# Last group of a four-sublayer kernel: value products made slot by slot, last feed-forward, bias and store in two halves

## What is computed

```python
# xn = layernorm(x); 16 heads of 64
q, k, v = xn @ wq * 64**-0.5, ctx @ wk, ctx @ wv
x = x + softmax(q @ k.T + mask) @ v @ wo
x = x + relu(layernorm(x) @ w1 + b1) @ w2 + b2        # w1 128x512, w2 512x128
```

## Time and profile before

| | before |
|---|---|
| median of three runs | 1377.8 us |
| the profiled execution | 1374.36 us, span 1372.4 us |
| TensorE matmul busy | 1290.7 us, 94% of the span |
| VectorE, ScalarE, GpSimd busy | 72%, 57%, 38% |
| mean granted TensorE clock | 0.976 |
| scores of tile 60 begin, last matmul ends | at 1306.2 us, at 1369.2 us |

### The profile page before, as it was taken

The page is one execution under the profiler, slowest core; times in us unless marked ns, Lnnn a source line. Parts: engine busy times, 40 slices in busy tenths (PEclk is TensorE's granted clock), DMA queues, the critical chain, the costliest instruction groups (busy, mean ns, idle before and its releaser), DMA issues.

```text
span 1372.4 us, 41789 instructions
## 1 busy us (share of the span) xinstructions
PE 1290.7 (94%) x16144; PEld 1136.1 (83%) x16145; DVE 986.1 (72%) x2428; ACT 780.1 (57%) x1482; POOL 517.5 (38%) x557
## 2 busy tenths in 40 slices
PE   4899999996999999988999999999999999999976
PEld 3788888875999999976788888888888888888866
DVE  3688888866655555537788788878877887788673
ACT  3455556642655555546656665666666666666632
POOL 2266666654122222247344324432443344332000
PEclk9899999998899999999999999999999999999988
DMA  3123242211422222221110111011101110110000
GB/s 104 45 74 128 76 137 78 76 68 64 137 76 77 76 77 77 65 77 39 29 33 13 31 35 33 14 31 35 33 14 29 37 31 15 29 37 14 8 4 16
DMA packets 86510, 71.06 MB, mean 52 GB/s; under 512 B 25072, under 2 KB 73200, under 8 KB 86352
## 3 DMA queue, kind: packets, MB, share of 16 engines
q1 hardware_dynamic: 74752, 42.71, 10.9%
q0 software_dynamic: 11600, 26.10, 6.0%
HBM read 40.73 MB, written 28.05 MB: 50 GB/s over the span
## 4 chain that ended last, share of the span: by engine, by line
PE 39%; DVE 10%; issue 3%; ACT 2%; POOL 1%; DMA 0%; DVEq 0%; POOLq 0%; ACTq 0%
PE c_ps_w L83 17%; PE c_ps_w L1566 7%; PE c_ps_w L1583 4%; PE c_ps_s L1532 4%; PE c_ps_w L1555 3%; PE c_ps_w L1541 3%; DVE c_r_max L1944 2%; DVE c_shifted L1942 2%; DVE c_shifted L1945 2%; PE c_ps_w L1463 1%; DVE c_probs L1957 1%; DVE c_xn_t_low L1867 1%; DVE k_ctx_t_low L898 1%; ACT c_o_t L1747 1%; ACT c_q_t L1719 1%
## 5 line engine op out<-in xcount | busy, mean ns | idle before, releaser
L1376 POOL TENSOR_TENSOR c_rstd<-c_var,c_minus_half 128x1 f32<-128x1 f32 x64 | 35.7, 558 | 353.7 <-DVE c_var L1925 353.6
L92 POOL DMA_INDIRECT sorted_x<-a_xn,f_slot_of x128 | 128.4, 1003 | 92.4 <-PE a_ps_w L767 36.0
L1566 PEld LDWEIGHTS c_ps_w<-c_wo,c_o_t 128*128 128x128 f32 x1024 | 125.1, 196 | 33.9 <-ACT c_o_t L1747 27.1
L1566 PE MATMUL c_ps_w<-c_wo,c_o_t 128*128 128x128 f32 x1024 | 130.9, 282 | 20.7 <-ACT c_o_t L1747 20.6
L1350 POOL DMA_INDIRECT c_back<-sorted_y,k_y_row_of x112 | 110.9, 991 | 102.2 <-PE c_ps_w L1555 52.9
L1109 PE MATMUL d_ps_y<-e_w_all,d_h_t 128*128 x1136 | 138.7, 276 | 0.0
L1109 PEld LDWEIGHTS d_ps_y<-e_w_all,d_h_t 128*128 128x128 f32 x1136 | 133.6, 193 | 0.0
L980 POOL DMA_DIRECT2D sorted_y<-d_y_rows x71 | 50.8, 716 | 208.6 <-DVE d_y_rows L1011 204.3
L1942 DVE TENSOR_TENSOR c_shifted<-c_ps_s,c_mask 128x1024 f32<-128x1024 f32 x64 | 78.3, 1224 | 57.8 <-PE c_ps_s L1532 57.7
L1719 ACT ACTIVATE c_q_t<-c_ps_w 128x512 f32<-128x512 f32 x120 | 70.2, 602 | 85.7 <-PE c_ps_w L83 84.7
L1058 ACT ACTIVATE d_h_t<-d_ps_h,d_biases 128x256 f32<-128x256 f32 x284 | 112.0, 476 | 2.5 <-PE d_ps_h L83 2.0
(11 more groups left out here) (250 smaller groups left out, 3554.7 us busy)
## 6 DMA issues: line engine op xcount, KB each, us to landing
d_x_rows<-sorted_x SPq DMA_DIRECT2D x71, 128.0 KB, 2.1
sorted_y<-d_y_rows POOLq DMA_DIRECT2D x71, 128.0 KB, 2.2
k_X<-in_x SPq DMA_DIRECT2D x16, 256.0 KB, 3.0
a_q_rows<-in_ctx SPq DMA_DIRECT2D x16, 256.0 KB, 3.3
ctx_cols<-a_q_t SPq DMA_DIRECT2D x16, 256.0 KB, 2.0
k_ctx_raw<-ctx_cols SPq DMA_DIRECT2D x16, 256.0 KB, 2.8
out<-k_X SPq DMA_DIRECT2D x16, 256.0 KB, 3.1
sorted_x<-a_xn,f_slot_of POOLq DMA_INDIRECT x128, 2.2
```

The source lines that it names most:

```text
L92: pool.indirect_dma_start(out=sorted_x, out_offset=bass.IndirectOffsetOnAxis(ap=slot_of[:, choice, t:t + 1], axis=0), in_=xn2[:, k, :], in ...
L1566: last = pe.matmul(w[:, 0:D], o_t[:, j, :], wo[:, j, :], start=(j == 0), stop=(j == J - 1))
```

## The change

Four edits to the end of `phase_c`.

1. `project_v` of tiles 60 to 63 moves from slots 56 to 59 into slots 60 to 63: the first half (`v, p, 0`) ahead of `transpose_probs(p - 1)`, the second behind it. ScalarE's `take_v` moves likewise. Slot p then makes the values that slot p + 1 uses.
2. The feed-forward of group 15 is made in halves of two tiles. The first half's transposes ("x4a") go into slot 63 between `values(62)` and `out_projection(62)`, its up products ("upa": two banks with two products of 256 columns each, three passes a product) behind `transpose_probs(63)`, its down products behind `values(63)`, ahead of `out_projection(63)`. The second half ("x4b", "upb", down 1) comes last.
3. POOL adds the bias of the last group in two halves of 128x256, the first ahead of `root4(63)`.
4. SP stores the last group in two halves of 128 KB, each when its `finish` is done.

At the end of slot 56 TensorE has the pair for tile 60 behind `out_projection(55)`; slot 57 has the pair for tile 61, slot 58 for tile 62 (each one ahead of the projection and one behind it), slot 59 for tile 63 (both ahead of it).

The diff, cut to its core (the changes of `filled` and of the slot conditions repeat those of TensorE's loop):

```diff
@@ tensor, loop over slots
-                coming = g + 1 < G
+                coming, early, last = g + 1 < G, g + 2 < G, g + 1 == G
...
+                if last:
+                    project_v(p, (0,))
                 transpose_probs(p - 1)
+                if last:
+                    project_v(p, (1,))
...
+                if k == 1 and early:
                     project_v(p + GT, (0,))
...
-                if k == 3 and coming:
+                if k == 3 and early:
                     project_v(p + GT, range(2))
+                if k == 3 and last:
+                    last_transposes("x4a", 0)
                 out_projection(p - 1)
...
             transpose_probs(NT - 1)
+            last_up("upa", 0)
             values(NT - 1)
+            last_down(0)
             out_projection(NT - 1)
-            x4_transposes(G - 1)
-            feed_up(G - 1, range(HC))
-            for half in range(2):
-                feed_down(G - 1, half)
+            last_transposes("x4b", 1)
+            last_up("upb", 1)
+            last_down(1)
@@ tensor, new functions
+            def last_up(name, half):
+                emptied(("x4a", "x4b")[half], G - 1)
+                HW = GW // 2
+                for n in range(HC // 2):
+                    w = begin(name, G - 1, n)
+                    for a in range(2):
+                        j = 2 * n + a
+                        last = split_matmul(pe, w[:, a * HW:(a + 1) * HW], f1, xn_t, ...)
+                    last.then_inc(full, 1)
+            def last_down(half):
+                for n in range(HC // 2):
+                    emptied(("upa", "upb")[half], G - 1, n)
+                w = begin("down", G - 1, half)
+                for n in range(GT // 2):
+                    k = half * GT // 2 + n
+                    for j in range(HC):
+                        last = pe.matmul(w[:, n * D:(n + 1) * D], h_t[:, j, k * P:(k + 1) * P], f2[:, j, :], ...)
+                last.then_inc(full, 1)
@@ scalar
             take_probs(NT - 1)
+            take_last_hidden("upa", 0)
             take_values(NT - 1)
-            high_x4(G - 1)
-            take_hidden(G - 1, range(HC))
+            high_last("x4b", 1)
+            take_last_hidden("upb", 1)
+            def take_last_hidden(name, half):
+                act.wait_ge(full, full_at("down", G - 2, 1))
+                for j in range(HC):
+                    act.wait_ge(full, full_at(name, G - 1, j // 2))
+                    ins = act.activation(h_t[:, j, half * HW:(half + 1) * HW], ..., ACT.Relu, bias=fb1[:, j:j + 1])
+                    if j % 2 == 1:
+                        ins.then_inc(free_of(name, G - 1, j // 2), 1)
@@ vector
+                if k == 3 and g + 1 == G:
+                    low_last("x4a", 0)
                 add_attention(p - 1)
             normalise_x4(NT - 2)
+            finish(G - 1, 0)
             add_attention(NT - 1)
             normalise_x4(NT - 1)
-            low_part("x4", G - 1)
-            for half in range(2):
-                finish(G - 1, half)
+            low_last("x4b", 1)
+            finish(G - 1, 1)
@@ gpsimd
+            add_last_bias(0)
             root4(NT - 1)
-            add_bias(G - 1)
+            add_last_bias(1)
@@ sync
+            for half in range(2):
+                sp.wait_ge(y_ready, 2 * (G - 1) + half + 1)
+                ks = ds(GT * (G - 1) + half * GT // 2, GT // 2)
+                sp.dma_start(x_out[:, ks, :], X[:, ks, :]).then_inc(stored[(G + 1) % 2], 16)
```

More of the change, by code:

```diff
@@ L1216, in filled @@
             yield from (("pt", NT - 1, half) for half in range(2))
+            yield from (("upa", G - 1, n) for n in range(HC // 2))
             yield from (("pv", NT - 1, b) for b in range(NB))
+            yield ("down", G - 1, 0)
             yield ("o", NT - 1)
-            yield ("x4", G - 1)
-            yield from (("up", G - 1, j) for j in range(HC))
-            yield from (("down", G - 1, half) for half in range(2))
+            yield ("x4b", G - 1)
+            yield from (("upb", G - 1, n) for n in range(HC // 2))
+            yield ("down", G - 1, 1)
         def filled_in_slot(p):
             g, k = divmod(p, GT)
-            coming = g + 1 < G
+            coming, early, last = g + 1 < G, g + 2 < G, g + 1 == G
             if k == 0 and coming:
@@ L1255, in filled_in_slot @@
                 yield ("k", g + 1, 7)
+            if k == 2 and early:
                 yield ("v", p + GT, 0)
@@ L1263, in filled_in_slot @@
                 yield ("q", g + 1, 6)
+            if k == 0 and early:
                 yield from (("v", p + GT, h) for h in range(2))
-            if k in (1, 2) and coming:
+            if k in (1, 2) and early:
                 yield ("v", p + GT, 1)
@@ L1280, in free_at @@
             return NUMBER[name] // BANKS + 1
-        HIGHS = {name: n for n, name in enumerate(n for n in NUMBER if n[0] in ("xna", "xnb", "xn", "x4"))}
+        HIGHS = {name: n for n, name in enumerate(n for n in NUMBER if n[0] in ("xna", "xnb", "xn", "x4", "x4a", "x4b"))}
         block = ctx.enter_context(nc.Block())
@@ L1809, in _ @@
                     take_k(g + 1, (5, 6))
+                if last:
+                    take_v(p, (0,))
                 take_probs(p - 1)
+                if last:
+                    take_v(p, (1,))
                 if k == 0 and coming:
@@ L1842, in _ @@
                     high_ctx(g + 2)
+                if k == 3 and last:
+                    high_last("x4a", 0)
                 if k == 0 and coming:
                     take_q(g + 1, (6,))
+                if k == 0 and early:
                     take_v(p + GT, range(2))
-                if k in (1, 2) and coming:
+                if k in (1, 2) and early:
                     take_v(p + GT, (1,))
             take_probs(NT - 1)
+            take_last_hidden("upa", 0)
             take_values(NT - 1)
-            high_x4(G - 1)
-            take_hidden(G - 1, range(HC))
+            high_last("x4b", 1)
+            take_last_hidden("upb", 1)
         @block.vector
@@ L1915, in normalise_x, with low_last @@
                 normalise_rows(range(GT), GT * g)
+            def low_last(name, half):
+                dve.wait_ge(high_ready, HIGHS[name, G - 1] + 1)
+                cols = slice(half * GW // 2, (half + 1) * GW // 2)
+                dve.tensor_tensor(xn_t.low[:, cols], bank(name, G - 1)[:, 0:GW // 2], xn_t.high[:, cols],
+                                  ALU.subtract).then_inc(free_of(name, G - 1), 1)
             def add_attention(p):
```

40 lines of the change are left out of this document (33 added, 7 removed).

## The result

The changed kernel has a median of 1369.49 us over six runs (1367.7 to 1374.0), against 1378.11 for the kernel before (1377.33 to 1380.77, six runs): ratio 0.9936, interval 0.9917 to 0.9954. A second comparison gave 0.9943 (0.9930 to 0.9956). The forecast was 1368.9, with 1365.6 to 1372.9 around it.

The account below looks back on a forecast made before the run. TensorE bounds slots 56 to 59; later the softmax chain and half clock after holes do, then a serial tail. Terms -4.3 -1.0 -0.5 -0.8 +0.5 -0.35 -2.2 -0.2 = -8.9 us, median 1377.8 to 1368.9, range 1365.6 to 1372.9.

Parts of the forecast that it names:

- slots 56 to 59: Value products leave busy TensorE: saves 1.40, 1.40, 1.35 and 0.15 us, sum 4.3; slot 59 gets a 1.3 us hole.
- slot 60: Added products cost nothing, half the clock's gain returns: -1.0 us; sign: slots 60 and 61 are 9.1 to 9.9 long.
- slot 61: Added products cost nothing; half the gain from losing its cold scores is taken: -0.5 us.
- slot 62: Added products cost nothing; its partly cold projection becomes warm, whole gain taken: -0.8 us, bounds 0 and -0.8.
- slot 63: TensorE sets the time: pays 1.40, regains 0.85 by warm scores; +0.5 us, bounds +0.5 and +1.4.
- mid: End of tile 62's projection to end of tile 63's: TensorE without holes, warm, 7.4 us; -0.35, bounds -0.5 and +1.5.
- last: Last projection to the end, before the store: 10.4 us against 12.57 before; -2.2, bounds -1.8 and -4.8.
- store: Last add's end to span's end, store halved to 128 KB: -0.2 us, bounds 0 and -0.9.
- that rival: Slots 56 to 58 give little back: VectorE sets the pace, each saves 0.2, sum -5.4 us, 1372.4; chance 0.06.
- the softmax chain: Scores, VectorE passes, exponential, o_t copies, projection: no slot shorter than 9.07 us; added products lie beside it in slots 60 to 62.
- The two near rivals: All warm before the tail, warm down half: -11.6 us, 1366.2, chance 0.15; clock stays as it is: -5.05, 1372.7, 0.15.
- The slower one: Moved products lie in the late slots' path: +3.9 us, 1381.7; decides where the hole ahead of projection is below 1.4; chance 0.02.

Follow-up runs that it names:

- the variant with real products: Changed kernel with the last group's value products one tile ahead, in the holes: 98.4 us from tile 56's scores, ratio 0.9890 to the kernel before.
- the halves alone: Changed kernel without the value products' move, group 15's feed-forward, bias and store in halves: 109.0 us from tile 56's scores, ratio 0.9978 to the kernel before.
- the two variants with the products one ahead: Changed kernel, last group's value products one tile ahead, without and with down halves waiting later: 98.4 and 97.9 us from tile 56's scores, ratios 0.9890 and 0.9896.
- The late wait variant: Changed kernel, last group's down halves waiting for the second bank's relu only at the third hidden chunk: 101.8 us from tile 56's scores, ratio 0.9923.

## Why the prediction was right

The mechanism came out as forecast: what leaves TensorE where it never idles is given back, what is added where it idles costs nothing, slot 63 pays, and the clock decides the rest. The closeness of the medians, -8.6 measured for -8.9 forecast, is in part luck: the trace has -7.6, and the steps below miss it in both directions.

Step by step, forecast against the profile (difference to before):

| step | forecast | profile |
|---|---|---|
| slots 56 to 59 | -4.3 | -4.1 |
| slot 60 | -1.0 | -0.3 |
| slot 61 | -0.5 | -0.8 |
| slot 62 | -0.8 | -0.7 |
| slot 63 | +0.5 | +0.6 |
| mid | -0.35 | -0.5 |
| last | -2.2 | -1.4 |
| store | -0.2 | -0.4 |
| sum | -8.9 | -7.6 |

- **Slots 56 to 58.** TensorE was the bound, and what left it left the slot: 1.39, 1.36, 1.29. Slot 59 gave 0.09, the o_t copies being next, with a new hole of 1.26 against the 1.3 forecast. TensorE waited for VectorE nowhere in slots 57 and 58; that rival is out by these four numbers.
- **Slots 60 to 62.** That the added products lie beside the softmax chain is shown by the kernel before with dummy products, whose slots 60 to 62 are those of the variant with real products, 9.1, 9.1 and 10.4. The clock was taken as half recovered in slots 60 and 61, -1.5; it was -1.1, but not by halves: slot 61 got all of its 0.8 and slot 60 only 0.3 of 1.8. With 10.61 slot 60 misses the prediction's own sign, 9.1 to 9.9. The place was right: the 2.1 us hole of slot 60, and dummy products in it alone bring 9.14.
- **Slot 63** pays the 1.4 and regains 0.85 by its scores, as worked out; the variant that leaves this pair in slot 59 shows that the pair is all of it.
- **Mid** was 7.15 against 7.4 forecast. TensorE has no hole, as forecast. At full clock this part takes 6.25 without the halves, so they cost 0.9 here; the gain against before is the clock.
- **Last** is the term that was mis-sized most: -1.4 for -2.2, outside its own bounds of -1.8 and -4.8. The forecast took 10.4, between cold in all (10.75) and a warm down half (8.9). The part ran at half clock from the up products to the end, 11.2: the up products' start 3.54 after the projection and not 3.4, up 2.93 and not 2.7, the hole 0.98 and not 0.9, the down half 3.75 as worked out. So 0.45 of the miss is the cold sum itself, and 0.35 the choice of a value below it. The text's own argument, that the new hole between up and down speaks for staying cold, should have decided it.
- **The store** fell from 2.73 to 2.34 us for 256 and 128 KB, and in the nine other profiles with the half it was 2.26 to 2.34. The listed medians of 3.1 and 2.2 are over the whole span; from issue to landing the last store alone took 2.3 with 256 KB and 1.8 with 128. The estimate from the Trainium skill, "DMA: Bandwidth & Descriptors", section on the two cost components, 2.6 to 2.3, was nearer with its -0.3 than my -0.2. The Trainium skill gives that sum there for a DMA of GpSimd's path, and this store is SyncE's.

The two near rivals both were partly there: in the last part the clock stayed down, in slots 61 to 63 it was all up. The slower one fails at its condition, which only slot 63 meets. The forecast of 8.9 meets the 8.6 of the medians better than the 7.6 of the trace, and where that 1 us comes from isn't shown: the runs of one kernel spread by 1 to 6 us, the profiles differ by up to 8.6 us ahead of tile 56, and the one profile of the kernel before could be 0.7 from another, as the halves alone show.

What stays open: why the clock stayed up in the last part of the two variants with the products one ahead, behind holes of 2.12 and 0.98 us, with no dummy products, while it fell in five other kernels (six profiles) with the same two holes, in some ahead of the first up product and in some a few products later. The late wait variant (the cold stretch 0.8 us later) and the halves alone (cold in slot 61 behind the same 1.18) suggest that it matters where a hole lies in time and not only how long it is; no run varied the place alone.

## What to carry to other kernels

Work that waits for nothing is worth most where TensorE idles, and least where it is the bound: before a move, read for each slot which of the two it is, and leave the piece whose old place gives nothing back (tile 63's pair, 0.1 for 1.4). Fill the one long hole rather than add work somewhere in the same slot, since 1.4 us of filler ahead of the values left a hole of 2.1 behind them, and with it the half clock and its 1.5 us. A few dummy products in a free bank tell in one run how much of a tail is clock and how much is waiting.

## What the runs showed of the hardware that was not expected

- One hole of 2.10 us ahead of the projection of slot 60 put TensorE at 1.2 GHz for most of that projection (3.41 to 3.51 us for 2.02) in five profiles, and in a sixth, with the late wait, from 0.8 us later on (projection 2.75, next scores 1.98); two holes of 0.9 to 1.3 in the same slot didn't, in three profiles.
- A hole of 1.18 us ahead of slot 61's projection was followed by a projection at full clock in the kernel before (2.02) and by one mostly at half clock in the one with the halves alone (3.09), though both have the same work up to there.
- The same work ahead of tile 56 ended between 1260.7 and 1269.3 us in thirteen profiles of kernels that are the same up to there: two kernels that differ in their last 70 us by 1 us are told apart by the trace from a common mark, not by the span, and only where the clock fell at the same places.
- Half clock cost the kernel before 6.7 us of its last 112, in one profile each, as dummy products without any use brought that much back.
